# A log-uniform sampled-softmax loss: a semaphore for each gather group, label gathers mixed between x gathers, dots one behind each tile

## The reference: what is computed

```
true    = x . w[label] + b[label]    - log(expected(label))
sampled = x . w[s]     + b[s]        - log(expected(s))         for 1024 sampled ids s
sampled = sampled - 1e9              where s == label
loss    = logsumexp([true, sampled]) - true
```

## Time and profile before

| | |
|---|---|
| median of 3 runs | 83.03 us (82.94 to 88.99) |
| span of the profiled execution, first to last instruction | 79.0 us, 638 instructions |
| the profiled execution's own time, beside its span | not given by the page |
| PE busy | 42.1 us (53%) |
| DVE busy | 47.2 us (60%) |
| ACT busy | 46.3 us (59%) |
| POOL busy | 42.3 us (54%), 40 gathers among it |
| mean granted clock of TensorE | 0.838 of full speed |
| chain that ended last, by engine | issue 26%, PE 21%, DVE 18%, ACT 10%, POOL 9%, another core or an unknown queue 8%, DMA 5% |

### The profile page before, as it was taken

How to read it: one execution, slowest core, us unless ns; L and a number is a source line. 1 busy time by engine, 2 the same in 40 slices (tenths; PEclk the granted TensorE clock), 3 DMA queues, 4 the chain that set the end, 5 groups by cost and what they waited for, 6 DMA issues and landing times.

```text
span 79.0 us, 638 instructions
## 1 busy us (share of the span) xinstructions
PE 42.1 (53%) x139; PEld 27.1 (34%) x139; DVE 47.2 (60%) x148; ACT 46.3 (59%) x74; POOL 42.3 (54%) x49
## 2 busy tenths in 40 slices
PE   0002599871059969253905605903996796769000
PEld 0002167140047655041604205503573565537000
DVE  0698886780071682648080093622965999998950
ACT  6049996712293092896084023079619895999770
POOL 7578686736868668578776868664680000000000
PEclk9999999998555899999999555555557999999995
DMA  0822121222344575968548689779689100000000
GB/s 7 221 65 33 18 34 17 29 25 17 25 25 18 25 24 18 30 19 21 24 23 30 20 18 29 20 18 33 21 18 30 4 0 8 0 0 0 0 0 4
DMA packets 1715, 1.91 MB, mean 24 GB/s; under 512 B 944, under 2 KB 944, under 8 KB 1712
## 3 DMA queue, kind: packets, MB, share of 16 engines
q0 software_dynamic: 1280, 1.33, 42.7%
q1 hardware_dynamic: 432, 0.55, 2.6%
HBM read 1.87 MB, written 0.01 MB: 24 GB/s over the span
## 4 chain that ended last, share of the span: by engine, by line
issue 26%; PE 21%; DVE 18%; ACT 10%; POOL 9%; another core or an unknown queue 8%; DMA 5%; DVEq 0%
POOL w_rows L219 9%; PE psum L291 8%; DVE psum L512 7%; PE psum L289 7%; ACT psum L339 6%; PE psum L290 5%; DVE masks L404 5%; DMA w_rows<-after,rows 3%; DVE xT L420 2%; DMA id_cols<-ids 2%; DVE lowest L512 1%; ACT masks L311 1%; PE psum L244 1%; DVE prod L521 1%
## 5 line engine op out<-in xcount | busy, mean ns | idle before, releaser
L512 DVE CUSTOM_DVE_ANT_0 psum<-psum,masks 128x1024 f32<-128x1024 f32 x16 | 19.7, 1231 | 16.4 <-PE psum L291 9.1
L289 PE MATMUL psum<-wT_high,xT 128*128 128x512 f32 x32 | 16.4, 511 | 21.3 <-issue 10.5
L339 ACT ACTIVATE psum<-psum,lowest 128x1024 f32<-128x1024 f32 x16 | 17.2, 1077 | 7.7 <-issue 5.2
L219 POOL DMA_INDIRECT t_rows<-after,rows x16 | 16.9, 1058 | 6.5 <-issue 4.7
L219 POOL DMA_INDIRECT x_rows<-front,rows x16 | 15.8, 990 | 6.9 <-issue 4.0
L289 PEld LDWEIGHTS psum<-wT_high,xT 128*128 128x128 f32 x32 | 7.1, 222 | 27.5 <-issue 21.2
L291 PE MATMUL psum<-b_parts,ones 128*128 128x512 f32 x32 | 14.8, 463 | 0.0
L290 PE MATMUL psum<-wT_low,xT 128*128 128x512 f32 x32 | 14.7, 460 | 0.0
L311 ACT ACTIVATE masks<-sample_ids,neg_label 128x1024 f32<-128x1024 int32 x9 | 10.3, 1140 | 3.1 <-DMA sample_ids<-sample_row 3.1
L334 ACT ACTIVATE xT<-psum 64x256 fp32r<-64x256 f32 (+1 forms) x9 | 3.0, 349 | 13.7 <-remote 7.4
L317 ACT ACTIVATE masks<-masks,ln_big 128x1024 f32<-128x1024 f32 x9 | 10.3, 1142 | 0.1
(11 more groups left out here) (78 smaller groups left out, 33.2 us busy)
## 6 DMA issues: line engine op xcount, KB each, us to landing
sample_ids<-sample_row SPq DMA_DIRECT2D x1, 512.0 KB, 3.9
x_rows<-front,rows POOLq DMA_INDIRECT x16
t_rows<-after,rows POOLq DMA_INDIRECT x16
w_rows<-after,rows POOLq DMA_INDIRECT x8
id_cols<-ids SPq DMA_DIRECT2D x1, 20.0 KB, 1.7
out<-loss SPq DMA_DIRECT2D x1, 8.0 KB, 1.4
```

What stands on the lines that cost most here:

```text
L219: return pool.indirect_dma_start(dst, None, table, bass.IndirectOffsetOnAxis(ap=rows[:, col:col + 1], axis=0))
L289: nc.tensor.matmul(o, x, wT_high[:, part], start=True, stop=False)
L339: nc.scalar.activation(logits(t), logits(t), ACT.Exp, bias=lowest[:, 0, t:t + 1], scale=-1.0, accum_out=sums[:, t:t + 1]).then_inc(exp_ok, 1)
L512: V.tensor_tensor_reduce(out=logits(t), in0=logits(t), in1=masks[:, t, :], scale=1.0, scalar=3e38, op0=ALU.add, op1=ALU.min, accum_out=low ...
```

## The change

The x groups get nine semaphores instead of two and the label gathers 16 instead of four. GpSimd then waits for no landing. The label gathers 0 to 9 are issued in pairs ahead of the x groups 4 to 8, that is ahead of x tiles 6, 8, 10, 12 and 14; label gathers 10 to 15 follow at the end. A wait on TensorE and VectorE is for 16 (or 32) on the group's or tile's own semaphore. In VectorE's queue one dot stands behind each of tiles 1 to 13, two behind tile 14 and one behind tile 15.

```diff
-T_SEMS = 4
 ...
         def x_arrived(g):
-            return sum(16 * (b - a) for a, b in X_GROUPS[g % 2:g + 1:2])
+            a, b = X_GROUPS[g]
+            return 16 * (b - a)
 ...
-        x_in = [sem(f"x_in{k}") for k in range(2)]
-        t_in = [sem(f"t_in{k}") for k in range(T_SEMS)]
+        x_in = [sem(f"x_in{g}") for g in range(len(X_GROUPS))]
+        t_in = [sem(f"t_in{t}") for t in range(TILES)]
 ...
             for g in range(len(X_GROUPS)):
-                if g >= 2:
-                    pool.wait_ge(x_in[g % 2], x_arrived(g - 2))
+                if g >= 4:
+                    for t in (2 * g - 8, 2 * g - 7):
+                        gather(t_rows[:, t, :], after, LAB + t).then_inc(t_in[t], 16)
                 for t in range(*X_GROUPS[g]):
-                    gather(x_rows[:, t, 0:EMBED], front, MOV + t).then_inc(x_in[g % 2], 16)
-            for t in range(TILES):
-                if t >= T_SEMS:
-                    pool.wait_ge(t_in[t % T_SEMS], 16 * (t // T_SEMS))
-                gather(t_rows[:, t, :], after, LAB + t).then_inc(t_in[t % T_SEMS], 16)
+                    gather(x_rows[:, t, 0:EMBED], front, MOV + t).then_inc(x_in[g], 16)
+            for t in range(2 * len(X_GROUPS) - 8, TILES):
+                gather(t_rows[:, t, :], after, LAB + t).then_inc(t_in[t], 16)
 ...
-                pe.wait_ge(x_in[g % 2], x_arrived(g))
+                pe.wait_ge(x_in[g], x_arrived(g))
 ...
-                dve.wait_ge(x_in[g % 2], x_arrived(g))
-                dve.wait_ge(t_in[t % T_SEMS], 16 * (t // T_SEMS + 1))
+                dve.wait_ge(x_in[g], x_arrived(g))
+                dve.wait_ge(t_in[t], 16)
 ...
-            dots_behind = {8: 1, 9: 2, 10: 2, 11: 2, 12: 2, 13: 2, 14: 4, 15: 1}
 ...
-                for _ in range(dots_behind.get(t, 0)):
+                for _ in range(0 if t == 0 else 2 if t == TILES - 2 else 1):
                     dot(dots_done)
                     dots_done += 1
```

## The result

The changed kernel takes 94.4 us (median of 4 runs, 94.25 to 94.98) against 83.0 for the runs of before that it is compared with: ratio 1.139, interval [1.131, 1.147]. I had forecast 81.0 and a range of 78.8 to 85.5. It is slower, in the direction of rival C and far outside its price.

What follows compares the result with a forecast made beforehand. TensorE's late signals under the gathers, in a ring of three PSUM slots, were taken as the bound. Earlier stream end 1.6 us plus dots 0.43 gave 2.0: span 79.0 to 77.0, plus 4.0 is 81.0 us, range 78.8 to 85.5.

Steps and rivals of the forecast that it cites:

- rival C: Ring in tiles 1 to 9: a stream without pauses lengthens the lateness, 3.1 us more, 85.7 us; chance 0.17.
- The stream's end: POOL's gather stream, freed of 3.66 us of waits, ends 2.9 us earlier, near 56.4 instead of 59.3.
- The holds by masks: A VectorE mask holds a POOL gather that begins inside it; one more hold takes 0.6 us from the gain.
- The dots: VectorE's queue: dots one behind each tile take 3 dots off the path, gaining 0.43 us, with no wait added.
- all labels are covered: VectorE's dots: each label lands before its dot needs it at the profiled pace, so no wait is added.
- The semaphores: Waits on TensorE and VectorE stay as many; more semaphores cost 0.
- The pace under the stream: Tiles 1 to 9 take 4.0 us each, later ones 1.76; ending the stream 2.9 us earlier nets 1.6 us.
- the lateness: TensorE's signals to VectorE come late while gathers are in flight, 9.3 us for tile 4, and punctual without them.
- three slots: PSUM slots shared by the ring of score, lateness, reduction and exponential; each microsecond late costs a tile a third.
- a lateness over 10 us: Sign in tiles 1 to 9 that the forecast is wrong because the stream without pauses makes signals later.
- The step from span to time: Whole kernel: the 4.0 us by which median 83.03 exceeded the profiled span 79.0, added to the forecast span 77.0.
- rival A: Timed runs lack the lateness or end it otherwise; label gathers bound both kernels, dots waiting near the end: 82.1 us, chance 0.18.

Runs made afterwards that it cites:

- n5_scratch: Changed kernel with 65536 instead of 16384 bytes per partition for gather descriptors: 67.1 us, ratio 0.961 to the kernel before, on a chip without late signals.
- e4_own_sems: Kernel before with a semaphore of its own for each x group and label gather, all POOL waits kept: 86.4 us, against 86.6 before.
- e1: Kernel before with own semaphores and POOL's 19 waits on landings taken out, gather order and dots as before: 93.5 us, ratio 1.075.
- m1: Changed kernel without its 16 label gathers, the dots reading the x rows twice: 74.8 us.
- m5: Changed kernel with the 16 label gathers replaced by 16 direct DMAs of fixed rows from SyncE's queue: 75.4 us.
- m3_paced: Changed kernel with POOL held before bursts of label gathers until VectorE has reduced tiles 0, 2, 4, 6, 8, 10: 76.6 us, later 77.5 us.
- m2_fill: Changed kernel with six idle matmuls on TensorE behind each score, into a PSUM bank nobody reads: 111.6 us.
- set 3: Third set of experiments: early pause, balanced bursts, rests and larger descriptor area, on a chip where the kernel before took 69.9 us and signals were punctual.

## Why the prediction was wrong

**The stream's end: right in kind.** Gaps of 0.30 us throughout, last gather at 54.21 where I had 55.5. The holds by masks came out with the other sign: I had taken 0.6 us off the gain for one more, but VectorE stood idle and met the stream with fewer masks. Three gathers were held, by 0.65, 0.44 and 0.87 us, 2.0 in all, where the kernel before has five, 2.6 us in all.

**The dots: no wait added at this pace, and little cost or gain.** 94.3 us with the old places, 94.4 with the new ones. The gain of 0.43 us was not seen. That all labels are covered rests on the slow pace: in n5_scratch, at the fast one, VectorE waited for labels five times, 2.9 us in all. One gather there met a dot and was held by 0.05 us, within the 0.1 that I had given.

**The semaphores: right,** nothing (e4_own_sems, 86.4 us against 86.6).

**The pace under the stream: wrong, and this is the step that failed.** "A stream that ends 2.9 us earlier turns 2.9 us of slow pace into fast pace" took the pace of 4.0 us a tile as a property of the stretch, to be kept when the stream changes. It was set by the lateness, and the lateness depends on POOL's pauses, which I was taking away. Measured: one tile reduced by the end of the last gather (55.2 us) in place of eight (59.3 us), and one signal 25.9 us late.

**Rival C named the mechanism and missed its size.** I priced one more lateness of 9.3 us over three slots, 3.1 us; it took 13.4. The sign that I had named for C, a lateness over 10 us, is there. Two things were wrong in the price. The lateness did not grow by a share of what was seen: from score 1 on every signal of work done under the stream came only behind its end. And three slots do not share it, since a late signal of a pair of transposes holds the next score with a slot free (31.70 to 46.84 us). An estimate of the worst case was in my hands: reduction 1 behind the stream's end (59 us as before), fourteen more tiles at 1.76 us, and the 5.4 us from the start of reduction 15 to the end, 89 us in span. With the 1.98 us a tile that were measured it is the 92.4 that came out.

**The step from span to time: mis-sized.** I carried over 4.0 us from 79.0 to 83.03. In the runs that have both, time and span are 1.8 to 2.3 us apart (94.54 and 92.4; a run of before with a span of 79.0 took 81.18). The other 1.9 us were scatter between runs of before. This did not make the forecast fail; without it, it would have been lower still.

**What is shown and what isn't.** Shown, where there is lateness: taking POOL's waits out makes the kernel slower (e1 against e4); TensorE's signals are then late by up to 26 us and more, and the fast pace begins only behind the end of POOL's gathers and moves with it (e1, m1, m5), though some signals come earlier (39.64 and 45.94 us in the changed kernel); long pauses bring them through (m3_paced); more work on TensorE doesn't (m2_fill). Seen on three chips against one: the lateness depends on where or when the kernel runs, beside traces that lack increments. The chip is not told apart from the hour, and the single fast runs of before (76.5, 75.1 and 72.8 us) say that the lateness also differs between executions on one chip. Not shown: the mechanism, whether the lost records and the late signals have one cause, whether either is there without a recording, and whether a burst's length or its rest decides. Where signals are punctual the stand-in n5_scratch gained 3.9%, more than the forecast 2.4%; dots then wait on labels near the end, as in rival A.

## What to carry to other kernels

A wait that looks like pure loss on one queue can be what another engine's signals come through in; before taking it away, ask what the trace shows of signals that arrive late, and try the worst case in which all of them wait for the end. Where equal runs scatter and the trace lacks records, run the kernel on more than one chip before explaining its profile. With late signals, try to pace a long run of gathers by its consumer: 76 to 78 us on two chips where the median of the kernel before was 85 and 89 (its fastest runs there took 76.5 and 75.1, so the pacing gains on the usual run and not on the best), at the price of 2.6 and 5.1% that two kernels paced in this way cost where signals were punctual.

## What the hardware showed that I had not expected

A signal of TensorE came 25.9 us behind the modelled end of its matmul, and its record in the trace is as late. VectorE's and ScalarE's were on time in the same stretch: ScalarE's cast ended at 46.34 and VectorE began at 46.37, VectorE ended at 46.79 and TensorE began at 46.84. In the phase of the first eight gathers TensorE's were on time as well: in the kernel before the last punctual one belongs to work that ended at 15.31 us, the first late one (by 2.65 us) to work that ended at 16.29, near the tenth gather. The page of the same program has a granted clock of 0.79 and a span of 92.1 us on one chip, and in set 3 (with the enlarged descriptor area) 0.95 and 65.2 us. A gather that begins inside a mask of VectorE takes longer than 0.94 us by what is left of the mask, less 0.12 or 0.13 us: 0.97 for 1.09 us left (before), 0.87 for 1.00 and 0.44 for 0.56 (the changed kernel).
